# Step 0's keys and values ahead of the queries in a Perceiver block on one core

## The chip, the core and the metric

One NeuronCore of a Trainium2 chip. The time is that of one execution on the device in microseconds (us), the median of three runs; the profile is of one further execution.

## What is computed

```python
x = x + xattn(layernorm(x), ctx_1024)      # 32 x 32 x 512 queries on 32 x 257 context rows, 16 heads
x = x + attn(layernorm(x))                 # FFT bind and unbind, sum over the 32 positions
x = x + ffn(layernorm(x))                  # 8 experts, one per token, gelu

# the cross attention, on which the change works
Q = query @ Wq.T + bq; K = key @ Wk.T + bk; V = value @ Wv.T + bv
scores = einsum('bhqd,bhkd->bhqk', Q, K) / sqrt(32)
weights = softmax(where(mask == 0, -inf, scores))
out = einsum('bhqk,bhkd->bhqd', weights, V) @ Wo.T + bo
```

Everything is float32 at the interface. Matrix products run as three float16 passes (high x high, high x low, low x high), so that most operands are split first: ScalarE writes the high half (`hi`), VectorE the low half (`lo`).

## The kernel before

The program is written engine by engine, each block in its own fixed order, with counting semaphores between them. Nothing reorders it: an instruction that waits holds everything behind it on its engine, and the SP block is the order in which all large loads are issued.

The context has 257 rows per batch item; the kernel works in 16 **steps** of two items. A step on TensorE is four key projections (`k_proj`, 12 matmuls of 512 columns each), the attention of the step before (L1480), the scores (`scores`, L1493) and four value projections (`v_proj`). Steps 1 to 15 are a loop (`pe.Fori`, L1529); step 0 is written out (L1528) and has no attention. The 257th context row of all items is projected apart, ahead of the steps: its keys (`klast`, L1415 to L1419) and its values (`vlast`, one product of 32 rows by 512 columns, L1420). The values go to HBM and back (L364, L367) to be spread over partitions, and `vl_cur`, a 128-row tile of which rows 0 to 31 are in use, holds those of one step (L504). The softmax is on VectorE (`scores`, `maxima`, `reciprocals`, `p_lo`) and ScalarE (`exp`, `p_hi`); the two weight tiles of a step are transposed by DMA (L377) before the next step's attention.

Ahead of the steps stands the **prologue**. In order on TensorE: the transposes of four layer-normalised token tiles (L1380), queries 0 to 2 of 8 (12 matmuls each; the first two are written out at L1398 and L1404), the other four transposes, queries 3 to 7, the last row's keys and values, and the product of the value bias with Wo (L1423), which VectorE adds to `bo` in `bias_tile` (L946). GpSimd computes the layer norm's power (L450), clears `vl_cur` (L456), and makes the high halves of the queries (L460). A query n takes the way ScalarE L646 (`q_f32`), GpSimd L460 (`q_hi`), VectorE L912 (`q_lo`), through two buffers: ScalarE's copy n waits for the low half of n - 2 (`q_lo`, n - 1).

SP issues x and Wq first, then constants, Wk, the last row, Wv, `bo` and Wo, then the context of step 0 when Wq is split (L349) and of step 1 when Wk is (L351); after the prologue's weights it issues the three mixing weights (L355) and nine small constants (L360), of use only later.

## Time and profile before

| | us |
|---|---|
| median of 3 runs | 820.86 (819.5 to 821.14) |
| the profiled execution | 814.98 |
| its span, first to last instruction | 813.2 |
| TensorE busy in it | 776.4 (95%) |
| VectorE busy | 627.3 (77%) |
| ScalarE busy | 468.5 (58%) |
| GpSimd busy | 232.8 (29%) |
| mean share of TensorE's full clock | 0.986 |

Start times in the profile are from the start of the span. "Busy" of TensorE counts modelled ends of pipelined matmuls, so a busy TensorE can still be one at half its clock. The chain of waits is followed back from the last instruction, each step to what released it; the timeline is in order of time. The profiled execution was 5.9 us shorter than the median; a gain or loss read from its rows is taken over to the median unchanged.

### The profile page before, as it was taken

How to read it: one execution, taken by the hardware profiler on the slowest of the kernel's cores; microseconds unless marked ns; L12 is line 12 of the kernel's file. 1: busy time of each engine (PE TensorE's matmuls, PEld its weight loads, DVE VectorE, ACT ScalarE, POOL GpSimd, SP SyncE). 2: the span in 40 equal slices, each digit the busy share in tenths (PEclk: the TensorE clock that was granted, in tenths of full speed). 3: DMA queues.
4: the chain of work that ended last, by engine and by line, in shares of the span. 5: the costliest groups of instructions: out<-in, count | busy, mean ns of one | idle time of the engine just before them, and what ended most of it. 6: DMA issues, size and time to landing. Idle time of an engine off the chain costs nothing.

```text
span 813.2 us, 22094 instructions
## 1 busy us (share of the span) xinstructions
PE 776.4 (95%) x8816; PEld 461.4 (57%) x8816; DVE 627.3 (77%) x984; ACT 468.5 (58%) x838; POOL 232.8 (29%) x411
## 2 busy tenths in 40 slices
PE   4999999999999999999999999996899999999995
PEld 2544555554555454555456545545768866876782
DVE  6867878888887887776768668787887789779760
ACT  2726655657665666555557034246577768767850
POOL 0421444333444333443322200004044222321220
PEclk9999999999999999999999999997899999999998
DMA  9353234442334443224523511102899998898510
GB/s 331 134 203 67 70 86 100 107 106 53 81 79 106 106 107 58 76 79 107 121 55 56 208 48 56 52 1 97 318 387 411 405 348 312 327 363 316 190 32 15
DMA packets 93745, 125.56 MB, mean 154 GB/s; under 512 B 76030, under 2 KB 78910, under 8 KB 82416
## 3 DMA queue, kind: packets, MB, share of 16 engines
q1 hardware_dynamic: 91104, 117.65, 45.0%
q0 software_dynamic: 2576, 7.02, 2.3%
q8 instruction: 44, 0.72, 0.4%
q14 instruction: 21, 0.17, 0.1%
HBM read 100.47 MB, written 6.88 MB: 132 GB/s over the span
## 4 chain that ended last, share of the span: by engine, by line
PE 85%; DVE 9%; ACT 3%; DMA 2%; issue 1%; POOL 1%; POOLq 0%; DVEq 0%; ACTq 0%
PE bank L1367 62%; PE bank L1701 10%; PE bank L1480 4%; PE bank L1673 3%; PE bank L1493 2%; ACT arena L705 2%; DVE arena L1004 2%; DVE arena L856 2%; DVE arena L1010 1%; PE bank L1380 1%; DMA arena<-arena 1%; ACT arena L622 1%; PE bank L1660 1%; DVE arena L1026 1%; PE bank L1404 1%
## 5 line engine op out<-in xcount | busy, mean ns | idle before, releaser
L1367 PE MATMUL bank<-arena 128*128 128x160 f16 (+8 forms) x4064 | 586.1, 304 | 8.7 <-DVE arena L856 2.9
L1367 PEld LDWEIGHTS bank<-arena 128*128 128x128 f16 (+3 forms) x4064 | 333.7, 100 | 249.6 <-issue 12.5
L622 ACT ACTIVATE arena<-arena 128x256 f16<-128x256 f32 (+4 forms) x293 | 251.0, 905 | 29.0 <-PE bank L1673 18.2
L856 DVE SCALAR_TENSOR_TENSOR arena<-arena 128x2048 f16<-128x2048 f32 (+2 forms) x95 | 199.3, 2121 | 23.7 <-ACT arena L622 23.1
L622 ACT ACTIVATE arena<-bank 128x512 f16<-128x512 f32 (+1 forms) x175 | 101.2, 586 | 155.2 <-PE bank L1367 124.4
L856 DVE SCALAR_TENSOR_TENSOR arena<-bank,arena 128x512 f16<-128x512 f32 (+1 forms) x174 | 117.7, 684 | 58.1 <-ACT arena L622 54.2
L1701 PE MATMUL bank<-arena 128*128 128x512 f16 x384 | 88.0, 380 | 0.0
L705 ACT ACTIVATE arena<-arena 128x257 f32<-128x257 f32 x128 | 63.5, 498 | 26.7 <-DVE arena L1012 26.7
L504 POOL TENSOR_TENSOR arena<-arena 32x1024 f16<-32x1024 f32 (+1 forms) x16 | 33.0, 2066 | 148.9 <-PE bank L1480 145.5
L1701 PEld LDWEIGHTS bank<-arena 128*128 128x128 f16 x384 | 35.5, 98 | 40.0
L521 POOL COPY arena<-arena 32x256 f16 (+1 forms) x128 | 50.3, 393 | 24.0 <-DVE arena L856 11.8
L1004 DVE SCALAR_TENSOR_TENSOR arena<-bank,arena 128x257 f32<-128x257 f32 x128 | 53.5, 480 | 0.0
L1026 DVE SCALAR_TENSOR_TENSOR arena<-arena 128x256 f16<-128x256 f32 x128 | 53.2, 476 | 0.0
L1304 DVE SCALAR_TENSOR_TENSOR arena<-arena 128x320 f16<-128x320 f32 x64 | 30.1, 489 | 26.3 <-ACT arena L622 26.3
L815 ACT ACTIVATE arena<-bank 128x320 f32<-128x320 f32 x64 | 27.2, 425 | 39.7 <-PE bank L1367 39.7
L569 POOL DMA_INDIRECT out<-arena x16 | 17.6, 1100 | 100.5 <-DVE arena L1296 98.1
L783 ACT ACTIVATE arena<-bank,arena 128x512 f32<-128x512 f32 x24 | 16.5, 686 | 46.6 <-PE bank L1367 46.2
L578 POOL DMA_INDIRECT arena<-l_dram,arena x14 | 20.4, 1454 | 79.2 <-PE bank L1660 49.0
L1010 DVE TENSOR_REDUCE arena<-arena 128x4 f32<-128x1028 f32 x32 | 39.2, 1224 | 1.1
L490 POOL TENSOR_TENSOR arena<-arena 128x256 f16<-128x256 f32 (+1 forms) x64 | 37.9, 614 | 1.2
L1480 PEld LDWEIGHTS bank<-arena 128*64 128x64 f16 x1792 | 30.0, 113 | 7.0 <-issue 6.4
L450 POOL TENSOR_TENSOR arena<-arena 128x4 f32<-128x4 f32 (+1 forms) x7 | 6.5, 927 | 95.7 <-DVE arena L864 95.6
(102 smaller groups left out, 454.0 us busy)
## 6 DMA issues: line engine op xcount, KB each, us to landing
arena<-in_w SPq DMA_DIRECT2D x64, 1024.0 KB, 7.8
arena<-in_ctx_t SPq DMA_DIRECT2D x16, 1024.0 KB, 5.3
arena<-in_awt SPq DMA_DIRECT2D x3, 1024.0 KB, 7.1
l_dram<-arena SPq DMA_DIRECT2D x4, 512.0 KB, 3.6
x_dram<-arena SPq DMA_DIRECT2D x1, 2048.0 KB, 13.2
arena<-in_x_t SPq DMA_DIRECT2D x2, 512.0 KB, 4.5
arena<-in_wq_t SPq DMA_DIRECT2D x1, 1024.0 KB, 7.3
arena<-in_x_t SPq DMA_DIRECT2D x1, 1024.0 KB, 9.9
```

Source lines behind the costliest of these rows:

```text
L490: g.tensor_tensor(q_bd[n][:, :, b, :].rearrange("p c (r q) -> p c r q", r=2), qT[n][:, :, bass.ds(st * (PB * S) + b * S, S)].unsqueeze(2) ...
L504: g.tensor_tensor(vl_cur[0:LAST_ROWS], vl_all[:, bass.ds(m, 1), :].broadcast_to((LAST_ROWS, PAIRS, P)), diag.unsqueeze(2).broadcast_to((LA ...
L521: g.tensor_copy(attT[n][own, :, bass.ds(m * (PB * S), PB * S)] .rearrange("p c (b q) -> p c b q", b=PB), att_st[n][own, :, :, r % 2, :]).t ...
L622: return a.activation(dst, src, ACT.Copy, scale=scale)
L705: a.activation(sm[:, j, :], sm[:, j, :], ACT.Exp, bias=neg_max[:, j:j + 1], scale=ISD / (SX * SK), accum_out=score_sums[:, j:j + 1]).then_ ...
L856: return v.scalar_tensor_tensor(dst, src, scale, h, ALU.mult, ALU.subtract)
L1004: v.scalar_tensor_tensor(sm[:, j, :], bank[:, 0:L], bank[:, L:L + 1], mask_bias, ALU.add, ALU.add).then_inc(s["s_free"], 1)
L1010: v.reduce_max(row_max[:, js], sm[:, js, :], AX_X).then_inc(s["s_max"], 1)
L1026: v.scalar_tensor_tensor(p_hl[1][b][:, j - b * KC, :], sm[:, j, 0:LM], recip[:, j:j + 1], p_hl[0][b][:, j - b * KC, :], ALU.mult, ALU.subtract
L1367: last = m.matmul(out_ap, w, x, start=(n == 0), stop=(n == len(pairs) - 1))
L1480: last = m.matmul(BG[own, cols], w[:, own], x[:, at * HALF:(at + 1) * HALF], start=(n == 0), stop=(n == len(pairs) - 1))
L1701: last = m.matmul(BC[:], hid_hl[z][:, f, 0:P], w[u][:, g, :], start=(f == 0 and u + z == 0), stop=(f == FC - 1 and z == 1))
```

## The change

Wk and the context of step 0 are loaded first, in four pairs of quarters (one chunk of 128 contraction rows each), with a semaphore per pair, then Wv, then x and Wq. ScalarE and VectorE split each quarter as it lands. TensorE begins with 11 matmuls on a tile of ones (`FILLERS`), whose result nobody reads, then runs step 0's keys chunk by chunk over four banks (`first_keys`), step 0's values (`first_values`), with the first four token transposes before the last of these, then the queries. Step 0's scores stand between queries 5 and 6, and 6 and 7. The last row's values become 48 matmuls of 32 x 128 outputs that are written to the four quarters of the partitions. The product of the value bias with Wo is gone: `bv` is loaded twice as a single row, split into rows 32 and 64 of `vl_cur` by ScalarE and VectorE, and columns of the weight tile are set to the constant `SP_` so that the attention adds it. `bias_tile` is loaded directly from `bo`. Steps 1 to 16 are what they were.

Three places in the program's order, before and now. **GpSimd, the head of the program** (L450/L457 is the layer norm's power, L456/L463 clears `vl_cur`, L460/L469 is a query's high half, L490/L507 spreads a step's queries, L504/L521 a step's last values). Before:

```order
L450 TENSOR_TENSOR arena<-arena 128x4 [waits ln_var,chain_pool]
L450 TENSOR_TENSOR arena<-arena 128x4 [waits ln_var]
L456 MEMSET arena 128x1024
L460 CAST arena<-arena 128x512 [waits q_f32] x8
L465 MEMSET arena 128x128 [waits bias_done,last_lo,q_lo]
```

Now:

```order
L457 TENSOR_TENSOR arena<-arena 128x4 [waits ln_var,chain_pool]
L457 TENSOR_TENSOR arena<-arena 128x4 [waits ln_var]
L463 MEMSET arena 128x1024
L469 CAST arena<-arena 128x512 [waits q_f32] x4
L507 TENSOR_TENSOR arena<-arena 128x4x64 [waits last_lo,q_hi]
```

The memset stands where it stood, behind the power of the second half of the tokens; the spreading of step 0's queries moved up between the fourth and the fifth high half.

**ScalarE, around the first query's copy** (L646/L678). Before, where L622 is the split of Wq, the four transposed token tiles and Wk:

```order
L622 ACTIVATE arena<-arena 128x2048 [waits wq_landed]
L622 ACTIVATE arena<-bank 128x4x128 [waits tr_ps] x4
L646 ACTIVATE arena<-bank,arena 128x512 [waits q_lo,q_ps,bq_done]
L622 ACTIVATE arena<-arena 128x2048 [waits wk_landed]
```

Now, where L652 is the same helper, here for tokens, values 2 and 3, and the two bias rows:

```order
L652 ACTIVATE arena<-bank 128x4x128 [waits tr_ps] x4
L652 ACTIVATE arena<-bank 128x512 [waits proj_ps] x2
L652 ACTIVATE arena<-arena 1x1024 [waits consts_landed,last_zero]
L652 ACTIVATE arena<-arena 1x1024
L678 ACTIVATE arena<-bank,arena 128x512 [waits q_lo,q_ps,bq_done]
L652 ACTIVATE arena<-arena 128x16 [waits ab_split]
L678 ACTIVATE arena<-bank,arena 128x512 [waits q_lo,q_ps]
```

The two bias rows and their wait for `last_zero` (GpSimd's memset of `vl_cur`) are ahead of the first query's copy.

**SP, ahead of step 0's two transposes** (L355/L369 loads a mixing weight, L360/L374 a constant). Before:

```order
L355 DMA arena<-in_awt 128x2048 [waits w_lo,tr_ps]
L355 DMA arena<-in_awt 128x2048 x2
...
L360 DMA arena<-in_quarter_offset 128x2
L364 DMA vlast_dram<-arena 32x512 [waits last_lo]
...
L382 DMA arena<-in_ctx_t 128x2048 [waits split_lo]
L377 DMA_TRANSPOSE arena<-arena 128x17x128 [waits p_last_ready,p_lo] x2
```

Now:

```order
L360 DMA vlast_dram<-arena 32x128 [waits last_lo]
...
L369 DMA arena<-in_awt 128x2048 [waits q_ps]
L369 DMA arena<-in_awt 128x2048 x2
...
L374 DMA arena<-in_quarter_offset 128x2
L385 DMA_TRANSPOSE arena<-arena 128x17x128 [waits p_last_ready,p_lo]
L385 DMA_TRANSPOSE arena<-arena 128x17x128 [waits p_last_ready,p_lo,q_lo]
```

The twelve loads moved from the middle of the prologue to directly ahead of the transposes, behind a wait for the last query's product.

The diff, cut to its core:

```diff
@@ banks
+        FIRST_PROJ = (BA, BB, BE, BC, BD, BA, BB, BC)
+        Q_BANKS = (BA, BB, BA, BB, BA, BB, BA, BG)
@@ SP
+            for k in range(KC):
+                sp.dma_start(wk_stage[:, k], i["wk_t"][:, k]).then_inc(s[f"first_landed{k}"], 16)
+                sp.dma_start(ctx_stage[0][:, k], i["ctx_t"][0][:, k]).then_inc(s[f"first_landed{k}"], 16)
+            sp.dma_start(wv_stage, i["wv_t"]).then_inc(s["wv_landed"], 16)
             sp.dma_start(x_tok[:, 0:2], i["x_t"][:, 0:2]).then_inc(s["x_landed0"], 16)
...
+            sp.wait_ge(s["q_ps"], 2 * KC)
             for n in range(3):
                 sp.dma_start(wt_stage[n], i["awt"][n].rearrange("p k c d -> p (k c) d")).then_inc(s[f"wt_landed{n}"], 16)
@@ GpSimd
+            for n in range(KC):
+                query_hi(n)
+            pool.wait_ge(s["q_hi"], KC)
+            pool.wait_ge(s["last_lo"], 2)
             queries_of(0)
-            step(0)
+            query_hi(KC)
+            query_hi(KC + 1)
+            last_block_constants()
+            pool.wait_ge(s["bv_lo"], 1)
+            last_values(0)
+            query_hi(KC + 2)
+            last_keys(0, 0)
+            query_hi(KC + 3)
+            last_keys(0, 1)
+            queries_of(1)
@@ ScalarE, first_step
+                v_first(3)
+                act.wait_ge(s["last_zero"], 1)
+                act.wait_ge(s["consts_landed"], 16 * (7 + HC))
+                for rows in (B, 2 * B):
+                    hi(vl_cur[rows:rows + 1].rearrange("p (b c) x -> p b c x", b=PB),
+                       bv_stage[rows:rows + 1].unsqueeze(1).broadcast_to((1, PB, KC, P)), SX).then_inc(s["bv_hi"], 1)
+                act.wait_ge(s["bq_done"], 1)
+                query(0)
...
+                query(3)
+                query(4)
+                query(5)
+                exp(0, 0)
+                query(6)
+                p_hi(0, 0)
+                exp(0, 1)
+                query(7)
@@ VectorE, first_step
+                for c in range(KC):
+                    k_first(c)
+                dve.wait_ge(s["consts_landed"], 16 * (7 + HC))
+                v.tensor_scalar(bq_scaled, bq_col, SX, None, ALU.mult).then_inc(s["bq_done"], 1)
+                token_stats(0)
+                v_first(0)
+                normalise(0, xhat0)
+                v_first(1)
+                weight_lo(1, wq, wq_stage)
...
+                tokens_lo(lnT_tile, 0, range(HT))
+                v_first(2)
+                v_first(3)
...
+                token_stats(1)
+                query_lo(0)
+                normalise(1, xhat0)
...
+                query_lo(3)
+                weight_lo(2, wo, wo_stage)
...
+                lo(ctx_hl[1][1], ctx_stage[1], SX, ctx_hl[1][0]).then_inc(s["split_lo"], 1)
+                dve.wait_ge(s["vlast_stored"], 2 * KC * 16)
+                for j in range(KC):
+                    scores(0, j)
+                maxima(0, 0)
+                query_lo(4)
+                reciprocals(0, 0)
+                query_lo(5)
+                for j in range(KC, PAIRS):
+                    scores(0, j)
+                maxima(0, 1)
+                query_lo(6)
+                p_lo(0, 0)
+                reciprocals(0, 1)
+                query_lo(7)
@@ TensorE
+            pe.wait_ge(s["fill_ready"], 1)
+            for _ in range(FILLERS):
+                m.matmul(BH[:], fill[:, 0:P], fill[:, P:], start=True, stop=True)
+            first_keys()
+            pe.wait_ge(s["w_lo"], 1)
+            for t in range(3):
+                first_values(t)
...
             transpose_tokens(0, xhat0, 0)
+            first_values(3)
...
+            for k in range(KC):
+                for u, z in ((0, 0), (0, 1), (1, 0)):
+                    for c in range(KC):
+                        last = m.matmul(BD[c * B:(c + 1) * B, 0:P], ctxl[u][:, k, :], wv[z][:, k, c * P:(c + 1) * P],
+                                        start=(k == 0 and u + z == 0), stop=(k == KC - 1 and u == 1))
...
-            split_product(BG[:], bv_bc, wo, lambda k: (slice(None), k, slice(None)),
-                          lambda k: (slice(None), k, slice(None))).then_inc(s["bias_ps"], 1)
...
-            step(0, prev=False)
+            scores(0, 0)
+            queries(range(KC + 2, KC + 3))
+            scores(0, 1)
+            queries(range(KC + 3, 2 * KC))
+            pe.wait_ge(s["q_f32"], 2 * KC - 1)
```


## Rows read from the trace of the kernel before

**Rows 1.** The page: TensorE's busy tenths and granted clock in 40 slices of the span.

```profile
PE   4999999999999999999999999996899999999995
PEclk9999999999999999999999999997899999999998
```

**Rows 2.** Chain of waits in order of time: start us, us, what.

```profile
14.31 3.57 PE bank L1398 x8
17.88 4.24 PE bank L1404 x16
22.13 2.59 PE bank L1367 x12
...
105.08 1.90 PE bank L1480 x112
...
129.48 0.53 PE bank L1480 x25
```

**Rows 3.** TensorE's timeline: start us, us, engine, line, op, operands, [idle before <-releaser].

```profile
9.89 3.65 PE L1380 MATMUL bank<-arena 128*128 128x128 f32 x16 [9.89 <-DVE arena L871]
14.31 3.57 PE L1398 MATMUL bank<-arena 128*128 128x512 f16 x8 [0.78 <-ACT arena L622]
...
24.55 1.91 PE L1380 MATMUL bank<-arena 128*128 128x128 f32 x16
...
70.16 10.53 PE L1367 MATMUL bank<-arena 128*128 x48 [1.66 <-DVE arena L856]
```

**Rows 4.** TensorE's timeline in the experts: the 32-row products of 128 columns.

```profile
604.53 0.85 PE L1673 MATMUL bank<-arena 128*32 128x128 f16 x48
```

**Rows 5.** Groups by line and shape, 0 to 90 us, ScalarE and VectorE: busy us, mean ns.

```profile
L622 ACT ACTIVATE arena<-arena 128x2048 f16<-128x2048 f32 x7 | 13.3, 1902 | 7.4 <-DMA arena<-in_wq_t 7.4
...
L856 DVE SCALAR_TENSOR_TENSOR arena<-arena 128x2048 f16<-128x2048 f32 x7 | 16.4, 2344 | 0.8 <-ACT arena L622 0.8
L856 DVE SCALAR_TENSOR_TENSOR arena<-bank,arena 128x512 f16<-128x512 f32 x23 | 15.3, 686 | 13.4 <-ACT arena L622 13.1
```

**Rows 6.** VectorE's timeline: the two layer norms, a softmax's start.

```profile
4.83 2.55 DVE L888 BATCH_NORM_STATS2 arena<-arena 128x6 f32<-128x512 f32 x4 [4.83 <-DMA arena<-in_x_t]
...
9.24 1.92 DVE L871 TENSOR_SCALAR arena<-arena 128x512 f32<-128x512 f32 x4 [1.24 <-POOL arena L450]
...
59.83 1.68 DVE L1004 SCALAR_TENSOR_TENSOR arena<-bank,arena 128x257 f32<-128x257 f32 x4
61.54 1.23 DVE L1010 TENSOR_REDUCE arena<-arena 128x4 f32<-128x1028 f32 x1
```

**Rows 7.** GpSimd's timeline in the prologue.

```profile
19.98 1.01 POOL L450 TENSOR_TENSOR arena<-arena 128x4 f32<-128x4 f32 x1 [10.78 <-DVE arena L864]
20.95 0.95 POOL L456 MEMSET arena<- 128x1024 f16 x1
21.84 0.80 POOL L460 CAST arena<-arena 128x512 f16<-128x512 f32 x1
```

**Rows 8.** Stretches of 5 us: PE, PEld, DVE, ACT, POOL busy (x count), granted clock, DMA share, GB/s.

```profile
15.00:20.00 5.00, 5.00 (x14) 1.76 (x13) 4.93 (x14) 0.00 (x0) 0.02 (x1) 1.00 1.02 401
...
555.00:560.00 5.00, 2.44 (x64) 2.11 (x62) 4.00 (x12) 4.94 (x7) 1.78 (x2) 0.87 0.62 206
560.00:565.00 5.00, 2.73 (x23) 2.21 (x24) 3.14 (x8) 3.29 (x5) 1.93 (x3) 0.50 0.00 0
```

**Rows 9.** TensorE's timeline where its clock fell.

```profile
560.13 1.03 PE L1586 MATMUL bank<-arena 128*128 128x128 f16 x8 [2.13 <-POOL arena L548]
```

**Rows 10.** SP's timeline: mixing weights, last small constant, last values' stores, step 0's transposes.

```profile
37.94 1.28 SPq L355 DMA_DIRECT2D arena<-in_awt  x3
...
43.78 1.27 SPq L360 DMA_DIRECT2D arena<-in_quarter_offset  x1
46.30 0.79 SPq L364 DMA_DIRECT2D vlast_dram<-arena  x2
...
71.53 7.14 SPq L377 DMA_TRANSPOSE arena<-arena  x2
```

**Rows 11.** Line L377 (the 32 transposes): us from issue to landing.

```profile
DMA to landing us min/median/max: 4.4/4.4/6.1
```

**Rows 12.** Tensor in_awt (three loads of 1 MB): us from issue to landing.

```profile
DMA to landing us min/median/max: 5.0/7.1/9.2
```

**Rows 13.** Tensor vlast_dram: us from issue to landing.

```profile
DMA to landing us min/median/max: 3.2/3.4/3.6
```

More of the change, by code:

```diff
@@ L665, in mixing_weights_hi @@
+            first_step()
             def mixing_weights_hi(k, n):
@@ L1066, in step @@
                     for j in range(KC, PAIRS):
-                        scores(j)
-                    maxima(1)
+                        scores(st, j)
+                    maxima(st, 1)
                 v_lo(2)
@@ L1399, in _ @@
             pe.wait_ge(s["tr_free"], HT)
-            pe.wait_ge(s["w_lo"], 1)
-            for n in range(2):
-                for k in range(KC):
-                    for u, z in ((0, 1), (1, 0)):
-                        last = m.matmul((BC, BD)[n][:], wq[u][:, k, n * P:(n + 1) * P], lnT[z][:, k, 0:D],
-                                        start=False, stop=(k == KC - 1 and u == 1))
-                last.then_inc(s["q_ps"], 1)
-            queries(range(2, 3))
+            for k in range(KC):
+                for u, z in ((0, 1), (1, 0)):
+                    last = m.matmul(BA[:], wq[u][:, k, 0:P], lnT[z][:, k, 0:D], start=False, stop=(k == KC - 1 and u == 1))
@@ L1448, in context_chunk, with scores, step @@
                 return ctx_all[:, bass.ds(st % 2 * 2 + z, 1), k, :].rearrange("p a x -> p (a x)")
-            def step(st, cur=True, prev=True):
+            def scores(st, b):
+                for c in range(0, KC, 2):
+                    pe.wait_ge(s["s_free"], from_zero(st * PAIRS + b * KC + c - 2))
+                    pe.sem_inc(s["pe_waits"], 1)
+                    tiles = [(c + odd, r, (r + odd) % 2) for odd in range(2) for r in range(2)]
+                    for n, (u, z) in enumerate(hl_passes(q_bd, kT)):
+                        for cc, r, at in tiles:
+                            rows = slice(r * HALF, (r + 1) * HALF)
+                            last = m.matmul(SCORE_BANKS[cc][at * HALF:(at + 1) * HALF, 0:L + 1], u[rows, cc, b, :],
+                                            z[rows, cc, b, :], start=(n == 0), stop=(n == 2))
+                    last.then_inc(s["s_ps"], 2)
+            def step(st, cur=True):
                 n0 = st * 8
```

432 lines of the change are left out of this document (224 added, 208 removed).

## Prediction

> **What bounds the kernel now.** I read four views in this order. The page's slices come first: TensorE is at 9 tenths in nearly every slice, with 4 in the first, and its granted clock is full but for two slices past the middle [rows 1]. So time is gained or lost where TensorE waits or does less. The chain of waits in order of time comes next. From step 2 on it stays on TensorE: the attention in step 2 starts at 105.08 us, the one in step 3 at 129.48, 24.40 later [rows 2]. The change leaves steps 1 to 15 alone, so the whole effect can be read at one mark, the start of the attention in step 2, **105.08 now**. Third, TensorE's timeline shows what lies ahead of the mark that isn't work [rows 3]: 9.89 us until the first transpose, 0.78 and 1.66 us of waits, and a slow start. The first 24 matmuls of 512 columns took 3.57 + 4.24 us, while 12 of the same shape take 2.59 afterwards [rows 2]; at 0.216 each, 24 are 5.18, so slowness cost 2.63. Their first eight take 0.45 each, the level of 1.2 GHz, the later ones that of 2.4 GHz. Sixteen float32 transposes took 3.65 us first and 1.91 later, 1.74 more. Work at full speed ahead of the mark is then 105.08 - 9.89 - 0.78 - 1.66 - 2.63 - 1.74 = **88.4 us**. Last come the other engines' rows, since the new order makes TensorE depend on their queues.
>
> **What is removed and added on TensorE.** The bias product (12 matmuls, 2.59) and the last row's values as 12 matmuls (2.59) go. The 48 matmuls of 32 x 128 that replace the latter have a twin in the experts: 48 took 0.85 [rows 4]. The projections, scores, queries and transposes keep their count. Work becomes 88.4 - 5.18 + 0.85 = **84.1**. The fillers are no part of it; they run before the data are there.
>
> **The start.** The first x load, 512 KB, let VectorE begin at 4.83 [rows 6]. The first pair of quarters is as large, so ScalarE can start near 4.7. A whole 128 x 2048 split takes 1.90 on ScalarE [rows 5], hence 0.5 per quarter, and the pair is split high by 5.8. Eleven fillers at 0.43 from about 1.2 end at 5.9. **TensorE's real work starts at 5.9** instead of 9.89. Pairs then land every 1.35 us at 401 GB/s [rows 8] and are split low in 1.2 us, while TensorE needs 2.59 per pair, so it doesn't wait for them. Quarters have 2 KB rows where x has 4 KB. No row shows such a load alone; I keep 401 GB/s, with up to 1.5 us of delay as the other bound.
>
> **The first wait, for query 0's copy.** I walk the queues with the durations of rows 5 to 7, each less the 0.1 us by which neighbours overlap. TensorE: keys to 16.2, three values to 24.0, transposes to 25.9, the fourth value to 28.5, query 0's high pass to 29.4. VectorE has no pause from the first key on, 15.7: four key halves to 18.2, the token statistics (2.55 plus 0.6 for aggregates) to 21.3, one value half, the normalisation (1.92, after GpSimd's 1.0) to 24.6, another value half to 25.2, Wq's low part (2.3) to 27.5, then four token halves to 30.1. So TensorE waits **0.9 us** for the token halves, then does queries 0 and 1 to 34.6. Query 2 needs query 0's copy out of the bank. On ScalarE that copy now stands behind the two bias rows, they behind the memset of `vl_cur`, which on GpSimd is behind the power of the second token half, and this waits for VectorE's second statistics. VectorE: two more value halves to 31.4, small sums to 31.9, statistics to 35.0. GpSimd: power 1.0 and memset 0.95 [rows 7], to 37.1. ScalarE: two rows of 1024 elements, half of the 2048 that take 1.90 each, to 39.1; the copy 0.7, to 39.8. TensorE waits 39.8 - 34.6 = **5.2 us**. If a single-partition row of 1024 is only as long as a 512-wide copy (0.6), it is 4.5; if GpSimd or VectorE run at the slow end of their contention, 6.
>
> **The second group of waits, around step 1.** From 39.8 TensorE does queries 2 to 7, four transposes, the last row and step 0's scores without a pause, to 60.9. VectorE meanwhile works off Wo's low part and step 1's context (2.3 each), which stand ahead of step 0's score reads. These start at 56.1; 1.68 and 1.23 us later [rows 6] the maxima are out; the exponentials end at 61.3, and query 6's copy, behind them on ScalarE, at 62.0: **1.1 us** of wait. The fourth key projection of step 1 needs a bank that VectorE frees behind the second half of the softmax, at 71.1: **1.4 us**. The last low halves of the weights are done at 72.8, and a transpose lands 4.4 us after its issue [rows 11], at 77.2; TensorE is there at 74.7: **2.5 us**. In the kernel before, the four value projections of step 0 cover this softmax; the queries that replace them cover it less, since each passes through the same three engines.
>
> **SP.** Twelve loads are now ahead of the first transpose on SP, behind a wait for the last query. Before, they took SP from 37.94 to 45.05 [rows 10], 7.1 us. From 61 that is until 68.2; the first transpose lands at 72.6, its reader comes at 73.7. It fits by one microsecond, so I cost it at nothing. What hides it is step 1's keys, and if their 10.4 us were shorter it would show. The transposes also share the queue with three megabytes, which took up to 9.2 us to land [rows 12]; the slowest transpose took 6.1 instead of 4.4 [rows 11]. Bounds: 0 to 1.7 us. I take 0, the median. By the Trainium skill, page "DMA: Bandwidth & Descriptors", section on queues, rings and completion order, each DMA engine consumes a queue's descriptors in ring order; by that alone the upper bound would hold and the sum would be 1.7 us worse.
>
> **Smaller edits.** The last values are ready at 49.1 in the walk; eight stores at 0.4 us, the last landing 3.4 after its issue [rows 10, 13], are over at 55.7, just ahead of VectorE's score reads at 56.1: costed at nothing, 0.5 us if one is late. Wo is issued when Wq is split, 27.5, and read at 40.4, and a megabyte took at most 9.2 [rows 12]. `bias_tile` is first read inside the steps. The bias now costs no matmul in the steps, as the weight tile's 128 rows were streamed anyway.
>
> **The sum.** 5.9 + 84.1 + 0.9 + 5.2 + 1.1 + 1.4 + 2.5 = 101.1, against 105.08: **4.0 us gained** if the clock stays full.
>
> **The clock.** It is granted at half once in the middle of the program: 0.87 of full in 555 to 560 us, 0.50 (1.2 GHz) in 560 to 565, where TensorE still shows 2.7 of 5 us busy [rows 8], and the longest single wait there is 2.13 [rows 9]. The new wait is 5.2 us with nothing at all on TensorE, so I expect the clock to fall in it and to be half when query 2 starts. The nearest price is the slow start, 2.63 for 24 matmuls; part of it is taken from the 1.1 us wait behind it, so I take **2.2 us**. Bounds are 0 and 4.4 (matmuls and transposes both slow, 2.63 + 1.74). The Trainium skill, page "TensorE: Matmul & The Clock Gate", Part 1, calls the throttled clock the default that activity releases, and idleness brings back. By that rule the wait costs twice, as here.
>
> Net: 4.0 - 2.2 = 1.8 us. Against the profiled execution, 814.98, that is 813.2; carried over to the median, 820.86 - 1.8 = **819.1**.
>
> **Rivals.**
> - *The clock survives the wait.* For it: it stayed full through waits of 0.8 to 1.7 us near 70 us [rows 3]. Against it: those are a third as long. Time: 820.86 - 4.0 = 816.9.
> - *The wait isn't there*, because VectorE reaches the second statistics earlier than walked or the small instructions are quicker. For it: nothing in the rows, only the walk's length. Then TensorE meets the later waits sooner and wins 2.8 of the 5.2: 4.0 + 2.8, 814.1.
> - *The head start isn't there:* quarters land late, or the fillers don't bring up the clock, which took until matmul 12 before [rows 2]. Price 1.5 to 2.6, say 2.0: 821.1, no change.
> - *The transposes sink in the weight loads* (the other side). Three megabytes ahead of them in one queue, both transposes at 6.1: TensorE's wait in step 1 grows from 2.5 to 4.2 us, and the clock falls a second time, 2.6 more. 820.86 - 1.8 + 1.7 + 2.6 = 823.4. It decides once the second transpose lands more than 5 us after TensorE is ready for it.
>
> **How the numbers follow.** Forecast 0.45, clock survives 0.22, no wait 0.05, no head start 0.15, transposes sink 0.13. What a measurement of this kernel can tell is about 0.2%, 1.64 us. The forecast, 1.8 with some 1.2 either way, is faster in 0.26, same in 0.17, slower in 0.02; with the rivals: faster 0.26 + 0.22 + 0.05 + 0.01 = 0.54, same 0.17 + 0.12 = 0.29, slower 0.17. The range runs from below the surviving clock, 815.0, to most of the sunk transposes, 823.2; outside are the case without a wait and the worst of the last rival.
>
> **What would show it.** Right: TensorE's first real matmul near 5.9; a pause of 4.5 to 6 us near 35 us, released by ScalarE's copy of query 0, with the two 1x1024 rows just ahead of it; a granted clock below 1 in 35 to 45; waits in step 1 for VectorE and the transpose; the mark near 103. Wrong: no pause near 35; a mark below 101 or above 105; a change in the 24.4 us between later steps, which nothing here accounts for.

## The result and the profile after

The changed kernel is slower: 826.62 us, median of 8 runs (824.66 to 831.22), against 819.97 of the kernel before (8 runs, 819.48 to 821.14). The ratio is 1.0086, with an interval of 1.0073 to 1.0099, some 7 us. The prediction had 819.1, in a range of 815.0 to 823.2.

| | before | after |
|---|---|---|
| the profiled execution | 814.98 | 826.74 |
| its span | 813.2 | 824.5 |
| TensorE busy | 776.4 | 781.4 |
| VectorE busy | 627.3 | 625.2 |
| GpSimd busy | 232.8 | 241.9 |
| mean share of TensorE's full clock | 0.986 | 0.976 |
| attention of step 2 starts (the mark) | 105.08 | 112.56 |
| from there to the attention of step 3 | 24.40 | 24.40 |

The chain of waits of the changed kernel in order of time, from the last wait ahead of the mark (start us, us, what), to set beside [rows 2]:

```profile
80.32 6.18 DMA arena<-arena
...
112.56 1.89 PE bank L1612 x112
...
136.96 1.00 PE bank L1612 x56
```

The mark is 7.5 us later, and the steps behind it have their old period. So the mark holds the whole loss, as the prediction wanted it read; the rest of the 11.3 us between the two spans lies in the experts and is not in the medians.

TensorE's granted clock in the page's 40 slices was low in the fifth slice too (82 to 103 us, in step 1), where [rows 1] had full tenths from the first slice to the middle:

```profile
PEclk9999799999999999999999999997899999999998
```

TensorE's timeline (start us, us, engine, line, operands, in brackets the idle time before it and what ended it). First the start:

```profile
6.26 1.24 PE L1483 MATMUL bank<-arena 128*128 128x512 f16 x4
7.33 1.89 PE L1490 MATMUL bank<-arena 128*128 128x512 f16 x8
```

The head start is there: the first keys begin at 6.26, at full speed (four matmuls in 1.24, eight in 1.89), where the kernel before did its first transpose at 9.89 [rows 3]. Then the prologue's middle and its end:

```profile
33.14 2.75 PE L1452 MATMUL bank<-arena 128*128 128x512 f16 x12
40.62 4.45 PE L1452 MATMUL bank<-arena 128*128 128x512 f16 x12 [4.72 <-ACT arena L678]
...
60.45 0.85 PE L1578 MATMUL bank<-arena 64*64 64x258 f16 x24 [3.77 <-POOL arena L511]
61.24 4.45 PE L1452 MATMUL bank<-arena 128*128 128x512 f16 x12
...
82.27 1.70 PE L1612 MATMUL bank<-arena 128*64 128x64 f16 x56 [2.74 <-DMA arena<-arena]
86.54 1.71 PE L1612 MATMUL bank<-arena 128*64 128x64 f16 x56 [2.57 <-DMA arena<-arena]
88.18 1.50 PE L1578 MATMUL bank<-arena 64*64 64x258 f16 x24
89.62 6.52 PE L1452 MATMUL bank<-arena 128*128 128x512 f16 x24
...
112.49 1.96 PE L1612 MATMUL bank<-arena 128*64 128x64 f16 x112
```

Four long waits stand in these rows: 4.72 for ScalarE's copy of query 0, 3.77 for GpSimd, 2.74 and 2.57 for two DMA transposes. Behind each, work is slow: 12 matmuls of 512 columns take 4.45 us, twice, and 56 small ones 1.70 and 1.71, where 112 take 1.96 at the mark. In stretches of 5 us around the first, the second and the last (busy of PE, PEld, DVE, ACT, POOL, then the granted clock):

```profile
40.00:45.00 5.00, 4.38 (x13) 1.72 (x14) 3.69 (x7) 3.05 (x4) 1.74 (x2) 0.66 0.00 0
60.00:65.00 5.00, 4.55 (x34) 2.00 (x35) 3.67 (x7) 0.71 (x3) 3.70 (x9) 0.66 0.01 3
...
85.00:90.00 5.00, 3.46 (x81) 2.61 (x82) 0.95 (x2) 0.60 (x1) 1.56 (x1) 0.50 0.43 177
```

What stands ahead of the first wait on the other engines is what the prediction named. ScalarE and GpSimd:

```profile
37.72 2.13 ACT L652 ACTIVATE arena<-arena 1x1024 f16<-1x1024 f32 x2 [7.42 <-POOL arena L463]
```

```profile
36.74 0.95 POOL L463 MEMSET arena<- 128x1024 f16 x1
```

What stands ahead of the second was not in the prediction. GpSimd spreads step 0's queries from 52.98 to 60.30 (a second copy, of 0.21, follows the rows here), while VectorE splits Wo and step 1's context (and the small `ab`):

```profile
52.98 3.74 POOL L507 TENSOR_TENSOR arena<-arena 128x256 f16<-128x256 f16 x2
56.66 2.36 POOL L511 COPY arena<-arena 128x8 f16<-128x8 f16 x1
58.97 1.18 POOL L507 TENSOR_TENSOR arena<-arena 128x256 f16<-128x256 f16 x2
```

```profile
53.54 5.41 DVE L917 SCALAR_TENSOR_TENSOR arena<-arena 128x2048 f16<-128x2048 f32 x3
```

The first of the same six instructions (four products and two copies) in the kernel before, where VectorE was idle (46.87 to 49.25) and then read a bank:

```profile
47.45 1.19 POOL L490 TENSOR_TENSOR arena<-arena 128x256 f16<-128x256 f16 x2
48.58 0.22 POOL L494 COPY arena<-arena 128x8 f16<-128x8 f16 x1
```

A copy of 128 x 8 took 0.22 us there and 2.36 here; all six took 2.6 us there and 7.3 here. The third place is SP, with step 0's transposes behind the mixing weights and the constants:

```profile
69.20 1.30 SPq L369 DMA_DIRECT2D arena<-in_awt  x3
...
75.56 0.73 SPq L374 DMA_DIRECT2D arena<-in_quarter_offset  x1
76.41 6.38 SPq L385 DMA_TRANSPOSE arena<-arena  x2
```

```profile
DMA to landing us min/median/max: 4.4/4.5/6.2
```

By these rows and the sum of the prediction, the 7.5 us at the mark divide as follows. "Slow clock" is what the groups took beyond the time of the same shapes at full clock.

| ahead of the mark | predicted | found |
|---|---|---|
| TensorE's real work starts | 5.9 | 6.3 |
| work at full speed (found: the remainder) | 84.1 | 84.5 |
| small waits ahead of the queries | 0.9 | 1.3 |
| query 0's copy | 5.2 | 4.7 |
| GpSimd's spreading | 0 | 3.8 |
| step 0's softmax (query 6, step 1's keys) | 1.1 + 1.4 | 0 |
| first, second transpose | 0, 2.5 | 2.7, 2.6 |
| slow clock (0.2 + 1.7 + 1.7 + 3.1) | 2.2 | 6.7 |
| mark | 103.3 | 112.5 |

### The profile page after: what moved, and what is told of

Read it like the earlier page. It is cut to its first block, busy times and chain, and to the rows that moved or that the text cites. A ratio compares the mean times of both kernels' runs of the same rounds, so it can differ in the third digit from the quotient of the medians.

```text
span 824.5 us, 22196 instructions
## 1 busy us (share of the span) xinstructions
PE 781.4 (95%) x8851; PEld 462.0 (56%) x8851; DVE 625.2 (76%) x989; ACT 471.5 (57%) x846; POOL 241.9 (29%) x413
## 4 chain that ended last, share of the span: by engine, by line
PE 78%; DVE 11%; ACT 4%; DMA 3%; issue 2%; POOL 2%; SPq 1%; POOLq 0%; DVEq 0%; ACTq 0%
PE bank L1452 57%; PE bank L1820 10%; PE bank L1612 4%; PE bank L1792 3%; DVE arena L917 3%; PE bank L1578 3%; ACT arena L685 2%; DMA arena<-arena 2%; DVE arena L973 2%; ACT arena L652 1%; DVE arena L979 1%; DMA arena<-in_wv_t 1%; DVE arena L995 1%; PE bank L1779 1%; POOL arena L507 1%
## 5 line engine op out<-in xcount | busy, mean ns | idle before, releaser
L1452 PE MATMUL bank<-arena 128*128 128x160 f16 (+6 forms) x4004 | 579.3, 305 | 14.0 <-ACT arena L678 4.7
L1452 PEld LDWEIGHTS bank<-arena 128*128 128x128 f16 (+1 forms) x4004 | 328.7, 100 | 252.8 <-issue 19.2
L652 ACT ACTIVATE arena<-arena 128x256 f16<-128x256 f32 (+4 forms) x301 | 254.0, 892 | 34.2 <-PE bank L1792 15.4
L917 DVE SCALAR_TENSOR_TENSOR arena<-arena 128x2048 f16<-128x2048 f32 (+5 forms) x101 | 200.3, 2012 | 35.3 <-ACT arena L652 31.6
L652 ACT ACTIVATE arena<-bank 128x512 f16<-128x512 f32 x175 | 100.0, 585 | 154.7 <-PE bank L1452 114.4
L917 DVE SCALAR_TENSOR_TENSOR arena<-bank,arena 128x512 f16<-128x512 f32 x174 | 116.7, 682 | 54.3 <-ACT arena L652 50.8
L521 POOL TENSOR_TENSOR arena<-arena 32x1024 f16<-32x1024 f32 (+1 forms) x16 | 32.9, 2059 | 146.7 <-PE bank L1612 146.5
L608 POOL DMA_INDIRECT arena<-l_dram,arena x14 | 24.6, 1756 | 77.5 <-PE bank L1779 47.3
L507 POOL TENSOR_TENSOR arena<-arena 128x256 f16<-128x256 f32 (+1 forms) x64 | 40.9, 660 | 1.2
L457 POOL TENSOR_TENSOR arena<-arena 128x4 f32<-128x4 f32 (+1 forms) x7 | 6.5, 927 | 111.4 <-DVE arena L925 111.3
L1612 PE MATMUL bank<-arena 128*64 128x64 f16 x1792 | 33.7, 199 | 5.6 <-DMA arena<-arena 5.5
```

The source lines that it names most:

```text
L507: g.tensor_tensor(q_bd[n][:, :, b, :].rearrange("p c (r q) -> p c r q", r=2), qT[n][:, :, bass.ds(st * (PB * S) + b * S, S)].unsqueeze(2) ...
L521: g.tensor_tensor(vl_cur[0:LAST_ROWS], vl_all[:, bass.ds(m, 1), :].broadcast_to((LAST_ROWS, PAIRS, P)), diag.unsqueeze(2).broadcast_to((LA ...
L652: return a.activation(dst, src, ACT.Copy, scale=scale)
L917: return v.scalar_tensor_tensor(dst, src, scale, h, ALU.mult, ALU.subtract)
L1452: last = m.matmul(out_ap, w, x, start=(n == 0), stop=(n == len(pairs) - 1))
L1612: last = m.matmul(BG[own, cols], w[:, own], x[:, at * HALF:(at + 1) * HALF], start=(n == 0), stop=(n == len(pairs) - 1))
```

## The experiments

Each ran beside the kernel before on its chip (three chips; the kernel before took 815.5, 819.8 and 815.0 us on them), so the ratios are what is compared. "Mark" is the timeline's start of the attention of step 2; it was 105.01 in the kernel before, and 112.49 in the changed one. Unless said, an experiment is the changed kernel with one edit. A mark comes from one profiled execution: with the fillers in place, query 1 starts between 32.94 and 34.07 us in these traces (33.14 in the changed kernel) though no edit touches what lies ahead of it but e1's memset, so differences of up to 1.1 us at the mark can come from the start alone.

| run | mark | ratio to before | interval |
|---|---|---|---|
| the changed kernel | 112.49 | 1.0086 | 1.0073 to 1.0099 |
| after_again, the same, other chip | 113.14 | 1.0081 | 1.0056 to 1.0106 |
| e1_clear_first | 107.01 | 1.0022 | 1.0013 to 1.0032 |
| e2_weights_after | 111.86 | 1.0059 | 1.0042 to 1.0076 |
| e3_hold_splits | 110.63 | 1.0064 | 1.0047 to 1.0080 |
| e4_all_three | 105.51 | 0.9993 | 0.9984 to 1.0003 |
| e5_constants_after | 110.05 | 1.0066 | 1.0050 to 1.0083 |
| e6_scores_first | 101.87 | 0.9953 | 0.9936 to 0.9970 |
| e7_order_alone | 107.84 | 1.0043 | 1.0029 to 1.0057 |
| e8_no_fillers | 112.95 | 1.0071 | 1.0053 to 1.0089 |
| e9_work_in_wait | 112.12 | 1.0083 | 1.0065 to 1.0101 |
| e10_work_in_transpose_wait | 100.54 | 0.9970 | 0.9959 to 0.9981 |
| e11_scores_first_no_fillers | 102.98 | 0.9978 | 0.9969 to 0.9988 |

### The first wait: e1_clear_first

```diff
+            g.memset(vl_cur, 0.0).then_inc(s["last_zero"], 1)
             power(0)
             power(1)
-            g.memset(vl_cur, 0.0).then_inc(s["last_zero"], 1)
```

> vl_cur is cleared ahead of both layer-norm powers instead of behind them; nothing else moves. Theory (three waits, each with a fall of the clock behind it): the 4.7 us wait of TensorE at 36 us and the half clock behind it go, query 2 starts near 35.7 instead of 40.6. Part of that is given back at the spreading of step 0's queries and at the transposes, so the attention of step 2 comes 3 to 6 us earlier than 112.5, at 106.5 to 109.5. Rival (the waits only move, since the softmax of step 0 is bound by VectorE, ScalarE and GpSimd and not by this wait): under 2 us earlier.

TensorE's timeline of it, to set beside the rows from 33.14 on above:

```profile
33.00 5.34 PE L1452 MATMUL bank<-arena 128*128 128x512 f16 x24
...
54.85 0.85 PE L1578 MATMUL bank<-arena 64*64 64x258 f16 x24 [3.78 <-POOL arena L511]
```

Queries 1 and 2 run on without a pause, and the mark comes 5.5 us earlier, within the 3 to 6 expected. The wait of 4.72 was set by one memset in the wrong place, by way of the two 1x1024 rows, and it cost its own length and a little of the clock. The other three waits stay as they were (3.78 in the row, 2.70 and 2.62 for the transposes), so they are no echo of the first.

### The transposes: e2_weights_after and e5_constants_after

```diff
                 if m + 3 < STEPS:
                     load_ctx(m + 3, (m + 1) % 2)
+                if m == 0:
+                    sp.wait_ge(s["q_ps"], 2 * KC)
+                    ...
```

The lines that follow are the removed ones of SP: for e2 the three mixing weights and the nine constants, for e5 the constants alone, with the weights left where they were.

> The three mixing weights and nine small constants are issued behind step 0's two transposes and the next context load, instead of ahead of them. Theory: the first transpose is issued at 72.9 instead of 76.4 and both land in 4.4 us instead of 5.9 and 6.2; the wait of 2.7 us for the first goes, the second's stays near 2.2 us since its weights are ready only at 78.3; the clock no longer stays at half for 10 us. Attention of step 2 4 to 6 us earlier, 106.5 to 108.5. Rival (the transposes are late because step 0's softmax is): the first's wait goes, the second's grows by as much, under 2 us earlier.

> Only the nine small constants go behind step 0's two transposes; the three mixing weights (3 MB) stay ahead of them. Theory A (issue time): the transposes are late because SP issues for 7.1 us ahead of them, 5.7 of it for the nine constants; then they are issued at about 70.6, the wait for the first one (2.7 us in the changed kernel) is gone, it lands in 4.4 us, and the mark falls by about 2 us, nearly as in e2_weights_after. Theory B (shared queue): the 3 MB ahead of them hold them up; then issue is earlier, but landing takes 6 us or more, and the first wait stays at 1 to 2.7 us. Time: 818 to 819 of a kernel before of 815.5 by A (1.004), 820 to 822 by B (1.006 to 1.008).

SP and the landing in e5_constants_after, where three loads of 1 MB are all that stands ahead:

```profile
72.96 9.76 SPq L379 DMA_TRANSPOSE arena<-arena  x2
```

```profile
DMA to landing us min/median/max: 4.4/4.5/9.4
```

```profile
82.37 1.07 PE L1612 MATMUL bank<-arena 128*64 128x64 f16 x56 [2.56 <-DMA arena<-arena]
```

and TensorE in e2_weights_after, where nothing stands ahead of them:

```profile
82.09 1.07 PE L1612 MATMUL bank<-arena 128*64 128x64 f16 x56
86.72 1.08 PE L1612 MATMUL bank<-arena 128*64 128x64 f16 x56 [3.56 <-DMA arena<-arena]
```

With the constants gone SP issued the first transpose 3.4 us earlier, at 72.96, and it landed when it had landed before: the longest landing of the kernel grew from 6.2 to 9.4 us, and TensorE's first wait was 2.56 instead of 2.74. SP was no sooner at the second transpose: issuing the first kept it until 80.2 in both kernels (7.25 us here, 3.79 in the changed kernel), 1.6 to 1.9 us past the point at which the second's weights were ready (78.27 in the changed kernel). The second then landed 4.7 us after its issue instead of 6.2; why is not shown, since e2 with nothing ahead had 6.1.

With the weights gone too, the first wait is gone. So the first transpose is late because of the three megabytes ahead of it in the queue, not because of SP's time to issue the constants; in e5 the last of them landed 9.8 us after its issue near 70.4, at 80.2, and the transpose 2 us later. That DMA engines take up a queue's descriptors in ring order is the rule that the prediction cited from the Trainium skill, page "DMA: Bandwidth & Descriptors"; this case's trace agrees with it.

The gain of e2, 0.27% or 2.2 us against the changed kernel, is smaller than the wait of 2.74, since the second transpose still kept TensorE waiting 3.56. At the mark of its one profile only 0.6 us of it show, where 4 to 6 were expected: that profile had a start 0.9 us later (query 1 at 34.07), and its first two falls of the clock cost more (query 2 took 5.30 us instead of 4.45, step 0's first scores and query 6 1.50 + 4.55 instead of 0.85 + 4.45). From the point at which the second's weights were ready, the second transpose landed 6.2 us later in e2 (80.48 to 86.67) and 8.2 us later in the changed kernel (78.27 to 86.50), and this 2.0 us fits the gain in time.

Of e5's two theories, A (issue time) falls and B (shared queue) holds in the wait. Its mark is 2.4 us earlier, 0.9 of it by the second transpose and the rest by less half clock; its gain in time (0.15 to 0.20% against the changed kernel) can't be told from none.

### GpSimd beside VectorE: e3_hold_splits, e4_all_three

```diff
                 query_lo(3)
+                dve.wait_ge(s["q_ready"], 1)
                 weight_lo(2, wo, wo_stage)
```

> VectorE waits for GpSimd's spreading of step 0's queries (q_ready) before it splits Wo and step 1's context. Theory (the two slow each other): GpSimd's four products and two copies at L507 and L511 take about 2.8 us in all instead of 7.5, TensorE's wait of 3.8 us ahead of step 0's scores goes, and with it the fall of the clock at 61 us. But VectorE's two splits end near 61, as now, so the softmax doesn't come earlier and most is given back as a longer wait ahead of step 1 or for the transposes: attention of step 2 0 to 2 us earlier than 112.5. Rival (GpSimd is slow here for another reason): the four products keep their 1.9 and the copies their 1.2 us, the wait stays, and the time grows by the VectorE time held, up to 4 us.

> The three edits together. Theory: the waits are in series and each edit removes its own, so the gains add up to more than the largest one: attention of step 2 at 99 to 103 us, the time 4 to 8 us under the kernel before. Rival (one bound, step 0's softmax chain, lies behind all three): no better than the best of the three alone by more than 1 us.

GpSimd and then TensorE in e3_hold_splits:

```profile
53.50 1.69 POOL L507 TENSOR_TENSOR arena<-arena 128x256 f16<-128x256 f16 x2
55.14 0.21 POOL L511 COPY arena<-arena 128x8 f16<-128x8 f16 x1
```

```profile
62.95 0.52 PE L1579 MATMUL bank<-arena 64*64 64x258 f16 x12 [2.27 <-DVE arena L973]
...
85.23 1.71 PE L1613 MATMUL bank<-arena 128*64 128x64 f16 x56 [4.19 <-DMA arena<-arena]
```

The spreading takes 3.1 us instead of 7.3, and the wait of 3.77 is gone, so the slow GpSimd was VectorE's doing. But the splits are now late, step 0's scores are read behind them, and TensorE waits 2.27 for the banks, 1.32 for a query's copy and 4.19 for the second transpose. The hold was paid back two places further on. By the Trainium skill, page "SBUF — State Buffer", section on who interferes with whom, a VectorE instruction with two SBUF inputs and a GpSimd instruction that reads SBUF exclude each other, and the one that comes second is blocked until the other ends. The rows agree: the 128x8 copy that began at 56.66 ended at 59.02, within 0.1 us of the end of VectorE's splits at 58.95.

The three single gains (0.64, 0.27 and 0.22% against the changed kernel) add up to 1.13%, and the three together gave 0.93%. So the gains nearly add, and more than the rival (one bound behind all three) allowed, but the mark of 99 to 103 and the 4 to 8 us under the kernel before that the theory expected did not come. That puts e4_all_three level with the kernel before, at a mark 0.5 us later, with 2.27 for the banks and 4.14 for the second transpose still there.

### VectorE's order: e7_order_alone, e6_scores_first

```diff
+                dve.wait_ge(s["split_hi"], 2)
+                lo(ctx_hl[1][1], ctx_stage[1], SX, ctx_hl[1][0]).then_inc(s["split_lo"], 1)
                 query_lo(3)
-                weight_lo(2, wo, wo_stage)
                 dve.wait_ge(s["ab_split"], 2)
                 lo(ab[1], ab_sd, SW, ab[0]).then_inc(s["ab_split"], 1)
-                dve.wait_ge(s["split_hi"], 2)
-                lo(ctx_hl[1][1], ctx_stage[1], SX, ctx_hl[1][0]).then_inc(s["split_lo"], 1)
                 dve.wait_ge(s["vlast_stored"], 2 * KC * 16)
                 for j in range(KC):
                     scores(0, j)
                 maxima(0, 0)
+                weight_lo(2, wo, wo_stage)
                 query_lo(4)
```

e7 is this edit alone; e6 has e1's and e2's as well, and not e3's hold.

> VectorE's new order of e6_scores_first alone, on the changed kernel: step 1's context split ahead of the fourth query's low half, Wo's behind the first four maxima; memset and SP's loads as in the changed kernel. If the order takes away the wait for GpSimd's spreading by itself: that wait falls from 3.77 us to 1.2 or less, with it the second fall of the clock (1.8 us), the mark at 108 to 109.5 and a ratio to the kernel before of 1.004 to 1.005. If most of the gain of e6_scores_first came from the other two parts, or needs them: mark 110.5 as in e3_hold_splits, ratio 1.006 to 1.007.

> The memset first and the loads behind the transposes, as in e4_all_three, but in place of the hold: VectorE splits step 1's context ahead of the fourth query's low half and Wo's low part behind the first four maxima, so that step 0's scores are read before Wo is split. Theory (VectorE's order is what delays step 0's softmax): the scores are read at about 54 instead of 56.7, TensorE's wait of 2.27 us for the score banks goes to under 0.5, the wait for the second transpose falls from 4.14 to about 3.4; mark near 102.5 to 103.5 and a time 2 to 3 us under the kernel before, ratio 0.9965. Rival (each place on VectorE costs someone): Wo's split slows GpSimd or holds the low half of query 4, a wait of 2 us appears elsewhere, and the mark stays at 105 to 106, ratio 0.999 to 1.000.

TensorE in e7_order_alone:

```profile
58.19 0.85 PE L1578 MATMUL bank<-arena 64*64 64x258 f16 x24 [0.48 <-POOL arena L511]
...
78.37 1.08 PE L1612 MATMUL bank<-arena 128*64 128x64 f16 x56 [1.34 <-DMA arena<-arena]
```

and VectorE and TensorE in e6_scores_first:

```profile
53.68 1.68 DVE L973 SCALAR_TENSOR_TENSOR arena<-bank,arena 128x257 f32<-128x257 f32 x4 [2.78 <-PE bank L1578]
```

```profile
53.02 0.85 PE L1578 MATMUL bank<-arena 64*64 64x258 f16 x24 [1.17 <-POOL arena L511]
...
77.08 1.71 PE L1612 MATMUL bank<-arena 128*64 128x64 f16 x56 [4.22 <-DMA arena<-arena]
...
101.87 1.96 PE L1612 MATMUL bank<-arena 128*64 128x64 f16 x112
```

Alone, the order takes the wait for GpSimd from 3.77 to 0.48, the first transpose's from 2.74 to 1.34, and the mark 4.7 us forward (the second transpose's wait grows from 2.57 to 3.43): 0.43% less, as expected or a little more, and about twice what the hold gave, though the two intervals overlap. The score reads begin 2.3 us earlier than in the changed kernel, and Wo is split in the time in which ScalarE takes the exponentials. Together with e1 and e2 the mark is 101.87, 3.1 us ahead of the kernel before, and the time is 0.47% under it (0.30 to 0.64%), the fastest version by its ratio (the intervals of e10 and e11, its variants below, overlap with its own). That mark is near the 101.1 to which the prediction's sum came with a full clock. Mark and time are better than expected (102.5 to 103.5, 0.9965), but the wait for the second transpose, 4.2 us, has not shrunk to 3.4 as the theory had it; TensorE gets there as much earlier as the weights do. In its chain (line, VectorE's low halves, then the transpose) the weights are ready at 71.40 and the transpose lands at 77.04, while TensorE is there at 72.9:

```profile
69.04 2.36 DVE arena L995 x4
...
71.45 5.59 DMA arena<-arena
```

In the kernel before, three of the four value projections, some 7.9 us, lay between step 0's first scores and step 1's keys (one between the two halves of the scores, two behind them; the prediction has all four cover the softmax). The change did them before, and two queries, 5.2 us, are what it put there.

### The clock: e9_work_in_wait, e10_work_in_transpose_wait

```diff
-            queries(range(1, 3))
+            queries(range(1, 2))
+            for _ in range(20):
+                m.matmul(BH[:], wq[0][:, 0, 0:P], lnT[0][:, 0, 0:D], start=True, stop=True)
+            queries(range(2, 3))
```

> The changed kernel with 20 matmuls of 512 columns (4.3 us) whose results nobody reads in the first wait of 4.72 us, ahead of query 2. The wait itself stays where it is, with 0.4 us left. Theory (the half clock behind the wait comes from TensorE having nothing to do, and is a price of its own): the 12 matmuls of query 2 take 2.6 us and not 4.45, the clock's first fall is gone from the records, and 1.9 us are gained up to there. The second and the third fall have their own waits and stay; whether the 1.9 us arrive at the mark depends on the wait for GpSimd, whose chain starts from query 3: mark 110.7 to 112.5, ratio 1.006 to 1.0085. Rival (the clock falls for another reason, such as the time since the start): query 2 takes 4.45 us as before, or the fall only moves behind the added matmuls; mark 112.5 or later.

e10 does the same with 17 matmuls in e6's last wait, in a step 1 that is written out ahead of the loop:

```diff
                 for b in range(PB):
+                    if b and fillers:
+                        pe.wait_ge(s["s_free"], PAIRS)
+                    for _ in range(b * fillers):
+                        m.matmul(BH[:], wk[0][:, 0, 0:P], wk[0][:, 0, :], start=True, stop=True)
                     pe.wait_ge(s[f"pt_landed{b}"], st * 16)
```

> e6_scores_first with TensorE's step 1 written out of the loop and 17 matmuls that nobody reads (3.7 us) in the wait of 4.22 us for the second transpose. If the clock falls for want of work: the fall at 76.8 is gone, attention, scores and the first values behind the wait go from 1.71 + 1.50 + 5.35 us to about 1.07 + 0.85 + 5.34, mark 1.3 to 1.6 us earlier, near 100.4, ratio 0.9935 to 0.995. If the added matmuls hold up the attention or the code written out costs something: mark 101.9 or later, ratio 0.9955 or more.

TensorE in e9_work_in_wait, then in e10_work_in_transpose_wait:

```profile
40.41 2.76 PE L1452 MATMUL bank<-arena 128*128 128x512 f16 x12 [0.41 <-ACT arena L678]
...
58.55 1.51 PE L1581 MATMUL bank<-arena 64*64 64x258 f16 x24 [3.77 <-POOL arena L511]
59.99 5.01 PE L1452 MATMUL bank<-arena 128*128 128x512 f16 x12
```

```profile
77.03 1.08 PE L1612 MATMUL bank<-arena 128*64 128x64 f16 x56 [0.34 <-DMA arena<-arena]
...
102.81 1.08 PE L1612 MATMUL bank<-arena 128*64 128x64 f16 x56 [1.20 <-DMA arena<-arena]
```

and the chain of e10 ahead of its wait of 1.20:

```profile
93.52 1.22 DVE arena L1082
...
96.95 5.82 DMA arena<-arena
```

Both show that the half clock comes from TensorE's having nothing to do. With work of no use in the wait, query 2 takes 2.76 us instead of 4.45, and the 56 matmuls behind the transpose 1.08 instead of 1.71.

Neither gain is left further on. In e9 the whole 1.9 us are there when step 0's scores start (58.55 instead of 60.45), behind the same wait of 3.77 for GpSimd; then the half clock behind that wait costs 1.2 us more (1.51 + 5.01 for scores and query 6 instead of 0.85 + 4.45), and the mark is 0.4 us earlier, the ratio the same. A second fall as long as that came in e2 too, without the added work, so one profile doesn't show that the work caused it. In e10 the mark is 1.3 us earlier, as expected, but the ratio of 0.9935 to 0.995 was missed (0.9970): step 2's attention waits 1.20 us for a transpose, and step 3's starts at 126.32, where it does in e6, at 126.27. That transpose is issued at 96.95, behind step 1's last low halves, and these are behind two sums of the mixing weights on VectorE (L1080, L1082). There the gain went into the next wait of the same kind.

### The fillers: e8_no_fillers, e11_scores_first_no_fillers

```diff
-FILLERS = 11
+FILLERS = 0
```

> The changed kernel without its 11 filler matmuls at the start. Theory (the fillers keep the clock up for the first keys): the first keys start at half the clock, 0.43 us a matmul instead of 0.216 for some 12 of them, and the mark is 2 to 2.6 us later, ratio to the kernel before 1.011 to 1.012. Rival (the records show a full clock from the start, and the first keys are anyway bound by the quarters that land): mark and time as in the changed kernel, 1.0086, or 0.3 us better.

> e6_scores_first without the 11 filler matmuls. In the changed kernel the fillers were worth 1.9 us on the first keys, but the mark hardly moved without them (112.95 to 112.49 and 113.14), since the first wait, for the copy of query 0, took the loss up. If that is so, here, where that wait is gone, the loss should arrive: mark 103.0 to 103.8 instead of 101.87, ratio 0.9965 to 0.998. If other waits (for VectorE's splits, 1.06 and 0.80 us, or for GpSimd, 1.17) take it up as well: mark within 0.5 us of 101.9, ratio 0.995.

> The changed kernel itself, on the same chip as the other experiments. If what was measured holds on this chip as well: 1.0086 of the kernel before (822.5 us to its 815.5), the mark at 112.5 with the same waits (3.8 for GpSimd, 2.7 and 2.6 for the transposes). If the loss depends on the chip: under 1.006, with other waits or other falls of the clock.

The start of e8_no_fillers:

```profile
6.03 1.86 PE L1483 MATMUL bank<-arena 128*128 128x512 f16 x4 [6.03 <-ACT arena L652]
7.69 3.20 PE L1490 MATMUL bank<-arena 128*128 128x512 f16 x8
```

Without fillers the first twelve matmuls take 1.86 + 3.20 us instead of 1.24 + 1.89, so the fillers do bring the clock up, for 1.9 us. Neither the 2 to 2.6 us nor the ratio of 1.011 to 1.012 that the theory expected for the mark and the time arrive: the mark is 112.95, beside 112.49 and 113.14 with fillers, and the ratio 1.0071. In e6's version (e11) the trace shows little: by the first values, at 18.79 us instead of 18.11, TensorE waits no longer for VectorE's splits, and the last wait ends at 77.38 instead of 77.08. The mark is 1.1 us later, as expected at the low end, but 0.8 of that is more half clock behind the last wait (24 matmuls in 6.17 us instead of 5.35), which these traces don't tie to the fillers. The ratio went from 0.9953 to 0.9978, 2 us, on another chip and with intervals that touch, so what the fillers are worth there lies between 0.3 and 2 us and is not settled. after_again bears the loss out on a second chip, with the same four waits, 4.72, 3.77, 2.62 and 2.83.

## Why the prediction was wrong

The sign was wrong: 1.8 us less was forecast and some 7 us more measured; at the mark, 103.3 was predicted and 112.5 found. The steps that failed are two terms that the sum put at nothing, GpSimd's spreading and the first transpose, each with a fall of the clock behind it. By its own steps:

- **The start, right.** 5.9 predicted, 6.26 found, quarters on time (in e2 and e3 a pair came 1.1 and 1.3 us late). What it is worth at the mark, less than thought: the first twelve matmuls end 1.7 us later in e8 and 1.9 in e11, and of that 0.8 and 0.4 are left when query 1 starts, as waits for VectorE's splits take up the rest.
- **The first wait, right in mechanism and size.** 5.2 predicted, 4.72 found, behind power, memset and two 1x1024 rows (2.13 us, walked as 2.0) that stood where the walk had them.
- **The clock, right at the first wait and wrong in number.** The first fall cost 1.7 us (4.45 less the 2.76 of e9), predicted 2.2; in the other runs with this wait query 2 took 4.21 to 5.30. But there were three, 6.5 us together. The sum charged the clock for one wait because it had no other long one; that waits near 1 us leave it full is right (0.89 and 1.17 in e6).
- **GpSimd's spreading, the step that was missing.** The prediction let VectorE "meanwhile" work off Wo's low part and step 1's context, and gave GpSimd's spreading beside them no term at all. The order of GpSimd's instructions was in the text ahead of it, and the room for it was named only for the power and the memset ("the slow end of their contention"). It cost 3.8 us of wait and a second fall of the clock, 1.7. Undisturbed it would have cost no wait: it began at 52.98 and takes 2.6 to 3.1 us, and TensorE came for it at 56.7.
- **The softmax waits of 1.1 and 1.4, not there.** They assumed that TensorE met VectorE's splits at full pace. Held up by GpSimd first, it found them done. Waits of this kind appear with the spreading quick: 2.27, 1.32 and 0.55 in e3, where the hold itself puts the splits about 3 us later, and 0.89 and 0.22 in e6 with the other order. So the mechanism is real, while its size with the splits in their old place is not shown.
- **The transposes, costed at nothing for the first.** "It fits by one microsecond" rested on a landing of 4.4 us from the issue. It took 5.8, and in e5, with an earlier issue, 9.4: what counts is when the megabytes ahead have drained. The other part is that the reader came sooner: 12.7 us behind the last query in the walk, 10.3 in the trace, because the two softmax waits that the walk had in between were not there. The prediction had this as its rival on the other side, with a chance of 0.13 and a price of 4.3 us. It cost 2.7 of wait and, with the second one's 2.6, a third fall of the clock, 3.1 us: 5.9 beyond the predicted 2.5. That the second wait is 2.6 where 2.5 was predicted is luck: its transpose landed 8.2 us after its weights were ready and not 4.4 (1.9 of it waiting for SP), and TensorE, itself late by the first, came 5.7 us after them and not 1.9. The condition given, a landing of the second transpose more than 5 us after TensorE is ready, was not met as put; it was the first that decided.

Both mechanisms of the last rival (late transposes, a repeated fall) came together with one that no rival had, and the range had room for one of the two at a time.

What stays open: whether a version exists in which the last wait of 4.2 us goes. It needs step 0's softmax some 4 us earlier or other work of TensorE's behind its scores; neither was tried.

## What to carry to other kernels

When work is moved forward on the bottleneck engine, list for every helper engine which instructions of the others now run beside it, and price it with rows that had that neighbour: here a 0.2 us copy became 2.4 us. Price a transfer behind others in its queue from the landing of the last load ahead of it, not from its own issue. And fix the place on the helper engine before filling a wait: moving one memset, twelve loads and two splits turned 0.9% of loss into 0.5% of gain, while work put into two of the waits kept the clock up there and brought nothing measurable in time.

## What the hardware showed that was not expected

- GpSimd instructions stretched to the end of a VectorE split from and to SBUF, or up to 0.5 us past it: 128x8 copy 0.22 to 2.36 us, the 128x512 cast 0.62 to 2.21 (e6, beside a split that began at 46.91). It goes the other way too, by less: in the changed kernel VectorE's first 128x2048 split, begun at 53.54 beside a product that had begun at 52.98, took 2.70 us, and the second, which began together with the copy, 2.28.
- Behind the same wait the half clock costs different amounts: query 2 behind the 4.72 took 4.45 us in the changed kernel, 4.21 in e5, 4.83 in e7 and 5.30 in e2. Whether it falls at all differs for waits of 2.3 to 2.8 us: behind 2.27 the scores ran at full clock in e3 and at half in e4, and behind the first transpose 56 matmuls took 1.07 us after 2.56 (e5) and 2.75 (e8), but 1.70 after 2.74 (the changed kernel) and 1.71 after 2.70 (e1). What decides was not settled.
- The issue of a DMA transpose on SP is itself held up behind loads: the longest took 3.79 us in the changed kernel and 7.25 in e5, where the median is 2.4; both ended at 80.2. With no loads ahead, the same one took 2.3 (e2).
